# Two quads' products with the values in one burst, ahead of the first head's turn

## The reference

```python
v = (values @ Wv + bv).reshape(N, L, H, D)      # H = 16, D = 32; values = keys = ctx
k = (keys @ Wk + bk).reshape(N, L, H, D)
q = (query @ Wq + bq).reshape(N, L, H, D)       # query = layernorm(x)
energy = jnp.einsum('nqhd,nkhd->nhqk', q, k)
energy = jnp.where(mask == 0, jnp.float32(-1e+20), energy)
attn = jax.nn.softmax(energy / np.sqrt(D), axis=3)
out = jnp.einsum('nhqk,nkhd->nqhd', attn, v).reshape(N, L, E)
return out @ Wo + bo                            # added to x
```

## Time and profile before

| what | value |
|---|---|
| three timed runs, median (lowest to highest) | 1930.35 us (1928.9 to 1932.52) |
| the profiled execution | 1930.36 us |
| its span in the trace | 1928.6 us |
| PE busy in the span | 98% |
| DVE, ACT, POOL busy | 67%, 54%, 41% |
| phase a, about | 0 to 660 us |

### The profile page before, as it was taken

How to read it: one execution, slowest core, us unless ns; L and a number is a source line. 1 busy time by engine, 2 the same in 40 slices (tenths; PEclk the granted TensorE clock), 3 DMA queues, 4 the chain that set the end, 5 groups by cost and what they waited for, 6 DMA issues and landing times.

```text
span 1928.6 us, 42677 instructions
## 1 busy us (share of the span) xinstructions
PE 1884.3 (98%) x13700; PEld 1446.0 (75%) x13700; DVE 1284.5 (67%) x3985; ACT 1032.7 (54%) x2674; POOL 798.1 (41%) x1482
## 2 busy tenths in 40 slices
PE   6999999999999999999999999999999989999998
PEld 5888888888888644444448888888888867787875
DVE  5887876767667678888865665656556566444475
ACT  5777767777777644644445544444454443222252
POOL 3454555656555545655543221322223133222264
PEclk9999999999999999999999999999999999999999
DMA  7343434443342767756552222121221236221131
GB/s 236 124 142 135 139 107 159 146 134 136 134 162 86 147 156 191 181 129 149 129 142 105 79 80 87 55 96 69 88 77 63 102 115 207 94 88 65 66 131 45
DMA packets 221532, 230.32 MB, mean 119 GB/s; under 512 B 123440, under 2 KB 139824, under 8 KB 221376
## 3 DMA queue, kind: packets, MB, share of 16 engines
q1 hardware_dynamic: 221376, 228.42, 38.7%
HBM read 144.47 MB, written 56.64 MB: 104 GB/s over the span
## 4 chain that ended last, share of the span: by engine, by line
PE 91%; DVE 3%; SPq 2%; DMA 2%; ACT 1%; issue 1%; POOL 0%; DVEq 0%; POOLq 0%; ACTq 0%
PE bank L1172 19%; PE bank L1158 18%; PE bank L2698 13%; PE bank L1868 10%; PE bank L1228 8%; PE bank L1243 6%; PE bank L1211 5%; PE bank L1913 5%; PE bank L1148 2%; DMA b_hqT<-b_hq 1%; SPq L1450 1%; PE bank L2601 1%; SPq L1456 1%; PE bank L2737 1%; DVE m_hrow L2532 0%
## 5 line engine op out<-in xcount | busy, mean ns | idle before, releaser
L582 POOL TENSOR_SCALAR a_probs<-a_probs,a_rinv 128x256 f32<-128x256 f32 x512 | 237.5, 483 | 270.1 <-DVE a_rinv L933 270.1
L711 ACT ACTIVATE a_probs<-a_probs,a_negm 128x256 f32<-128x256 f32 x512 | 254.7, 502 | 96.4 <-DVE a_negm L917 95.3
L582 POOL TENSOR_SCALAR c_probs<-c_probs,c_rinv 128x256 f32<-128x256 f32 x128 | 67.1, 534 | 371.8 <-DVE c_rinv L933 371.8
L917 DVE CUSTOM_DVE_ANT_0 a_probs<-bank,a_mbias 128x256 f32<-128x256 f32 x512 | 191.6, 416 | 7.5 <-PE bank L1211 6.8
L2698 PE MATMUL bank<-m_xnT,m_s 128*128 128x512 f32 x768 | 184.9, 392 | 2.7 <-DVE m_hid L2436 2.7
L926 DVE COPY a_pT<-bank 128x512 f32<-128x512 f32 x128 | 88.2, 689 | 135.8 <-PE bank L1228 135.6
L2698 PEld LDWEIGHTS bank<-m_xnT,m_s 128*128 128x128 f32 x768 | 142.8, 188 | 33.5 <-DVE m_hid L2436 3.1
L711 ACT ACTIVATE c_probs<-c_probs,c_negm 128x256 f32<-128x256 f32 x256 | 127.0, 500 | 75.0 <-DVE c_negm L917 75.0
L1228 PE MATMUL bank<-a_ident,a_probs 128*128 128x128 f32 x1024 | 154.8, 274 | 4.0 <-ACT a_pT L719 2.3
L1228 PEld LDWEIGHTS bank<-a_ident,a_probs 128*128 128x128 f32 x1024 | 121.9, 141 | 23.6 <-issue 10.8
L1730 ACT ACTIVATE b_hq<-b_hround 128x1024 bf16<-128x1024 f32 x64 | 67.2, 1052 | 124.2 <-POOL b_hround L1669 119.4
(11 more groups left out here) (287 smaller groups left out, 4323.1 us busy)
## 6 DMA issues: line engine op xcount, KB each, us to landing
kept<-a_cT SPq DMA_DIRECT2D x32, 512.0 KB, 5.4
m_ew<-in_L_ffn_w_dram SPq DMA_DIRECT2D x24, 512.0 KB, 8.7
a_cbuf<-in_ctx_dram SPq DMA_DIRECT2D x16, 512.0 KB, 5.5
a_xbuf<-in_x_dram SPq DMA_DIRECT2D x16, 512.0 KB, 4.7
a_resb<-in_x_dram SPq DMA_DIRECT2D x16, 512.0 KB, 4.1
b_part<-in_L_ffn_w_gate_dram SPq DMA_DIRECT2D x32, 256.0 KB, 2.9
b_part<-in_L_ffn_w_up_dram SPq DMA_DIRECT2D x32, 256.0 KB, 3.7
b_part<-in_L_ffn_w_down_dram SPq DMA_DIRECT2D x32, 256.0 KB, 4.2
```

The source lines that it names most:

```text
L582: last = nc.gpsimd.tensor_scalar(pr, pr, rinv[:, s, r:r + 1], 0.0, ALU.mult, ALU.add)
L711: nc.scalar.activation(pr, pr, ACT.Exp, bias=negm[:, s, h % 2, t:t + 1], scale=-1.0, accum_out=ssum[:, s, QT * (h % 2) + t:QT * (h % 2) + ...
L917: nc.vector.tensor_tensor_reduce(out=probs[:, s, h % 2, t], in0=s_bank[h][:, t * SEQ:(t + 1) * SEQ], in1=mbias[:, el.par], scale=-sm_scale ...
```

## The change

In phase a, quads 0 and 2 ("even") now begin with the scores of the next quad and with the products with the values of both quads before; the turn of the first head comes behind them. Quads 1 and 3 keep the turn first, then scores, and have no products with the values. The two quads of a burst write the two halves of `o_bank`, and ScalarE and VectorE take them out in even quads, two instructions each. On VectorE the copy of turn 0 moves in even quads from the front to behind the scores of head 0. The last batch does quad 2's products in quad 3 and quad 3's at the end, one by one. There two fillings change place, and a small product of phase b's weight sums moves from quad 2 to quad 3 of batch 5. Phase c (QUADS == 2) keeps its order.

```diff
-                 (2, 1): [("o0", (0,)), ("o1", (0,))], (2, 2): [("up", 0)], (2, 3): [("gate", 1)],
+                 (2, 1): [("up", 0)], (2, 2): [("o0", (0,)), ("o1", (0,))], (2, 3): [("gate", 1)],
...
+    def scores_lead(q):
+        return QUADS == 2 or q % 2 == 0
+
+    def quads_behind(el, q):
+        if QUADS == 2 or last_batch(el) and q == QUADS - 1:
+            return [quad_before(el, q)] if q > 0 or has_before(el) else []
+        if q % 2 or q == 0 and not has_before(el):
+            return []
+        pe, pq = quad_before(el, q)
+        return [(pe, pq - 1), (pe, pq)]
+
+    def burst_of(el, q):
+        apart = QUADS == 2 or last_batch(el) and q >= QUADS - 2
+        return (q, q) if apart else (q // 2 * 2, q // 2 * 2 + 1)
+
+    def attn_columns(q):
+        at = q % 2 * SEQ if QUADS == 4 else 0
+        return slice(at, at + GPQ * SEQ)
...
         def attn_hi(el, q):
-            act.wait_ge(pv_done, quads_upto(el, q))
+            act.wait_ge(pv_done, quads_upto(el, burst_of(el, q)[1]))
...
         def quad_of_16(el, q):
-            probs_out(el, q, 0)
+            if not scores_lead(q):
+                probs_out(el, q, 0)
...
             if more:
                 scores_out(ne, nq, 0)
+            if scores_lead(q):
+                probs_out(el, q, 0)
...
         def probs_v(el, q):
-            wait_for(pe, otlo_done, quads_upto(el, q) - 1)
+            if burst_of(el, q)[0] == q:
+                wait_for(pe, otlo_done, quads_upto(el, q) - 1)
...
                 for j in range(4):
-                    if j == 0 and QUADS == 2:
+                    if j == 0 and scores_lead(q):
                         if nq > 0 or el.has(1):
                             scores(ne, nq)
                         probs_v_before(el, q)
                     transpose_probs(el, q, j)
-                    if j == 0 and QUADS == 4:
+                    if j == 0 and not scores_lead(q):
...
-        return isinstance(el.n, int) and (el.n, quad) == (SCALES_AT, 2)
+        return isinstance(el.n, int) and (el.n, quad) == (SCALES_AT, 3)
```

More of the change, by code:

```diff
@@ L722, in attn_hi @@
         def attn_hi(el, q):
-            act.wait_ge(pv_done, quads_upto(el, q))
+            act.wait_ge(pv_done, quads_upto(el, burst_of(el, q)[1]))
             rows = turned_out(el)[:, HI, q * GPQ:(q + 1) * GPQ].rearrange("p g n -> p (g n)")
             if v_bias is None:
-                nc.scalar.activation(rows, o_bank[:, 0:GPQ * SEQ], ACT.Copy).then_inc(othi_done, 1)
+                nc.scalar.activation(rows, o_bank[:, attn_columns(q)], ACT.Copy).then_inc(othi_done, 1)
             else:
-                nc.scalar.activation(rows, o_bank[:, 0:SEQ], ACT.Identity, bias=cols[:, BV, q:q + 1]).then_inc(othi_done, 1)
+                nc.scalar.activation(rows, o_bank[:, attn_columns(q)], ACT.Identity, bias=cols[:, BV, q:q + 1]).then_inc(othi_done, 1)
         def attn_hi_before(el, q):
-            if q > 0 or has_before(el):
-                attn_hi(*quad_before(el, q))
+            for before in quads_behind(el, q):
+                attn_hi(*before)
         start = Element(0, 0, batches)
@@ L949, in attn_lo @@
         def attn_lo(el, q):
-            dve.wait_ge(othi_done, quads_upto(el, q))
+            dve.wait_ge(othi_done, quads_upto(el, burst_of(el, q)[1]))
             hi, lo = (turned_out(el)[:, part, q * GPQ:(q + 1) * GPQ].rearrange("p g n -> p (g n)")
@@ L953, in attn_lo @@
             if v_bias is None:
-                nc.vector.tensor_tensor(lo, o_bank[:, 0:GPQ * SEQ], hi.bitcast(F32), ALU.subtract).then_inc(otlo_done, 1)
+                nc.vector.tensor_tensor(lo, o_bank[:, attn_columns(q)], hi.bitcast(F32), ALU.subtract).then_inc(otlo_done, 1)
             else:
-                nc.vector.scalar_tensor_tensor(lo, o_bank[:, 0:SEQ], cols[:, BV, q:q + 1], hi.bitcast(F32),
+                nc.vector.scalar_tensor_tensor(lo, o_bank[:, attn_columns(q)], cols[:, BV, q:q + 1], hi.bitcast(F32),
                                                ALU.add, ALU.subtract).then_inc(otlo_done, 1)
         def attn_lo_before(el, q):
-            if q > 0 or has_before(el):
-                attn_lo(*quad_before(el, q))
+            for before in quads_behind(el, q):
+                attn_lo(*before)
         start = Element(0, 0, batches)
@@ L1242, in probs_v @@
                         c = slice(m * hd, (m + 1) * hd)
-                        last = nc.tensor.matmul(o_bank[c, i * SEQ:(i + 1) * SEQ],
+                        last = nc.tensor.matmul(o_bank[c, attn_columns(q).start + i * SEQ:attn_columns(q).start + (i + 1) * SEQ],
                                                 vb[:, el.par, kt, g * P + m * hd:g * P + (m + 1) * hd],
@@ L1249, in probs_v_before @@
         def probs_v_before(el, q):
-            if q > 0 or has_before(el):
-                probs_v(*quad_before(el, q))
+            for before in quads_behind(el, q):
+                probs_v(*before)
         if prior:
```

## The result

| | median, us | runs | profiled execution, us | its span, us |
|---|---|---|---|---|
| before | 1930.36 | 1928.9 to 1932.52 (4) | 1930.36 | 1928.6 |
| after | 1965.72 | 1964.08 to 1966.39 (4) | 1964.08 | 1962.3 |

The changed kernel takes 1.0181 of the time before, 95% interval 1.0163 to 1.0199. It is slower, as predicted, but by 35.4 us and not by 22.9. The median lies 4.7 us above the upper end of the range.

What follows compares the result with a forecast made beforehand. TensorE, busy 98% of the span, was taken to bound the kernel. Batches 1 to 14 (+21.6), the last batch (+3.0) and batch 0 (-1.7) sum to +22.9 on 1930.36: 1953.3 us, range 1945 to 1961.

Steps and rivals of the forecast that it cites:

- 14 x 1.54 = 21.6: Attention batches 1 to 14: each was taken to cost 1.54 us more, 21.6 us together.
- The batch: One steady batch of four quads: 1.91 - 0.20 + 0.83 - 1.00 = +1.54 us.
- T1: Second turn of quad 0: waits 0.61 us for VectorE's copy of the first turn, now behind the burst.
- o0: Output projection in quad 0: its first half waits 0.33 us for VectorE's low part of q1, behind the copy.
- T3: Last turn of quad 0: waits 0.12 us for VectorE's copy of the third turn.
- tx0's wait: Quad 1, product behind the scores: waits for VectorE's low part of tc1, starting about 2.1 us after the first turn, not 1.44.
- v0's: Quad 1, product behind tx0: waits for VectorE's rows of o1, leaving the quad only 0.20 us shorter, not 1.00.
- Quad 2: Quad 2 of a batch: longer by 0.83 us with the burst, its copy covered by half a projection.
- quad 3: Quad 3 of a batch: loses its products with the values, 1.00 us shorter, with no new wait.
- The saving of 0.16 per burst: TensorE work alone: joining two quads' products with the values saves 0.16 us per pair of quads, about 5 us over 31.
- The ends: Last batch +3 us (between +1 and +4) and batch 0 -1.7 us (between -3 and 0).
- The rival of the clock: TensorE's clock falls to half for 6.6 us once a batch behind the new waits: +46, 2000 us; chance 0.04.

Runs made afterwards that it cites:

- e1: Changed kernel plus 46 instructions of repeated fulfilled waits ahead of the first transposes, putting the loop at its old place: 1952.49 us, ratio 1.0110.
- e11: Changed kernel plus 23 instructions of repeated fulfilled waits ahead of the first transposes: 1952.78 us in one run.
- e2: Kernel before plus 150 instructions of repeated fulfilled waits in TensorE's first 14 us, order of work untouched: 1949.16 us, ratio 1.0101.
- e8: Changed kernel, loop at old place, VectorE's low part of q1 (k0 in quad 2) ahead of its copy of turn 0 in quads 0 and 2: 1948.73 us.
- e5: e3 and e8 combined, with the turn ahead of scores and burst on TensorE and VectorE's copy waiting for the burst's first half: 1933.51 us, ratio 1.0007.
- e3: Changed kernel, loop at old place, VectorE's low part of tc1 ahead of its copy of turn 0 in quad 1: 1941.89 us, ratio 1.0062.
- e6: Changed kernel with burst at quad 2 alone, loop at old place, VectorE's tc1 low part and o1 rows ahead of its quad 1 copy: 1928.64 us, ratio 0.9982.

## Why the prediction was wrong

The direction and the working of a batch held; the sum over the attention did not.

- **The failed step** is "Batches 1 to 14 give 14 x 1.54 = 21.6". It took every batch as the steady one and the cost of the loop's back edges as nothing, without a reason. Two of the fourteen hold a back edge and cost 6.6 and 6.3 us more, 13 us. The new order of work isn't the cause (e1, e11: same order, cost gone; e2: old order, a like cost there). The changed kernel has 46 fewer instructions ahead of the loop (counted in the program), and TensorE's code then comes again over the instruction queue: 14 packets of 16 KB between 366 and 516 us, where the kernel before had none. A packet holds 256 instructions, worked out so: TensorE executes 28,887 in the kernel before by its trace. Its loops repeat 1649 of them twice, 1131 five times and 723 once; without these repeats 19,211 are left, and 19,211 / 75 packets is 256.1. The loop has 1645 to 1649 instructions, 6.4 packets. It stays in place with starts 0, -6, -23 and +80 from that of before, and is fetched again at -46 and +150. A start of the kernel before 23 to 45 instructions into a packet would explain all six: the loop then touches 7 packets in the first four and 8 in the other two. That the place of the loop decides is shown; that the number of packets it touches is the reason is worked out from these six places, and the exact edges were not tried.
- In the Trainium skill, the page "Runtime: NRT & Kernel Launch", section "Instruction fetch mechanics", gives PE 128 KiB of instruction memory, refilled in 16 KiB blocks, and says that a taken branch to a page outside those held has to wait for a fetch. The runs agree in kind: packets of 16 KB come and TensorE idles 1.2 to 2.4 us at a time behind the branch. They don't bear out the size as a limit: 128 KiB are eight blocks, and a loop that touches eight, by the count above, was fetched again. The box in that section speaks of two cache lines with purely sequential prefetch; by that each of the loop's back edges would stall in every kernel here, and in the kernel before none does. The 75 packets of that kernel decide.
- **The batch** was predicted at +1.54 and measured at +1.44 (41.49 in e1, 40.05 before). By its parts: the waits of T1, o0 and T3 were predicted at 0.61 + 0.33 + 0.12 and show in the timeline as 0.55, 0.33 and 0.12 beyond the distances of the earlier trace rows; e8 took away 0.35, and e5 beyond e3 and that another 0.33 (0.68 - 0.35). tx0's wait and v0's behind it were predicted to swallow 0.80 of the 1.00 of quad 1; e3 gave back 0.62 and e6 0.20, together 0.82. Quad 2 was +0.83, measured +0.82; quad 3 -1.00, measured 8.50 against 9.50.
- **The saving of 0.16 per burst** was right: 0.18 in e6.
- **The ends** were put at +3.0 and -1.7. Measured are +1.0 behind the second turn of batch 15 and -0.9 up to that of batch 1. The 14 batches between take 20.5 us more in e1, whose loop is not fetched again (580.83 against 560.30), so the work itself costs 20.6 where 22.9 were foretold, most of the difference in the last batch and in the 0.10 per batch. That the median of e1, 1952.49, lies within 1 us of the forecast is thus in part luck.
- The rival of the clock priced half clock once a batch. It never fell behind the 0.44 to 0.61 us waits of a batch: in e1, which has them all, the granted clock is 1.00 over 100 to 640 us. In the changed kernel it fell at both back edges, with gaps of 1.57 + 2.41 and 1.89 + 2.40 us, and in e2 at the one with 1.51 + 1.20 us, each time in or right behind the second gap. At the other back edge of e2, with 1.70 + 1.48 us, it stayed at 1.00; what makes the difference is open.

The range failed with the sum: it held the spread of known terms, and the missing term was larger than all of it. What could have warned was there: in the kernel before the instruction queue brings no packet between 353 and 515 us, the loop's second and third iteration, so the loop stays in place there, and the change moves the number of instructions ahead of it.

## What to carry to other kernels

Moving work in a long loop also moves the code: compare the instruction packets (q8 here) and the idle time "issue" at the back edges before blaming the order, and shift the code by a few dozen instructions as a control. To join two short stretches of narrow products saved 0.12 to 0.18 us here, and what they covered has to be covered by something else: list for each bank which other engine empties it, and in which order that engine's queue stands. Here VectorE's order in quad 1 alone was worth 0.82 us a batch, more than four times the saving.

## What was not expected of the hardware

- Two kernels that do the same work in the same order differ by 13 us of 1950 (0.65%) by 23 instructions in the place of TensorE's loop (1965.72 against 1952.78, one run of e11; 46 instructions give the same, 1952.49 in four runs of e1).
- The two back edges with fetches cost 6.6 and 6.3 us after the change: 4.0 and 4.3 us are idle time, and most of the rest goes with the clock (0.51 over 366 to 373, 0.57 over 458 to 462). In e2, where the clock stayed at 1.00, 3.2 us of idle time cost 3.4.
- A wait that is fulfilled already isn't free on TensorE: with 46 instructions of two such waits each the first transpose starts at 6.71 us (e1), with 70 of them at 9.33 us (e2), so an instruction takes about (9.33 - 6.71) / 24 = 0.11 us. With 23 of them (e11) the start is hidden behind the transfer, at 4.60 us.
